# Where the count matrix of the last graph layer is turned: on TensorE, or by the transfer that loads it

## The reference

```python
def _L3_gnn_ref(x, edge_index, W, b):
    row, col = edge_index[0], edge_index[1]
    h = x @ W + b
    agg = segment_sum(h[col], row, num_segments=n)
    deg = segment_sum(ones, row, num_segments=n)
    return agg * where(deg > 0, 1 / deg, 0)[:, None]
...
x = _layernorm(x + _L3_gnn_ref(x, edge_index, W, b))
```

## Time and profile before

| | us |
|---|---|
| three executions, median | 3149.36 |
| profiled execution | 3150.74 |
| its span (first to last instruction) | 3149.1 |
| layers, to the end of the last product of `sum_rows` | 2938.4 |
| seam: from there to the last feature tile | 2938.4 to 2968.2 |
| rest of the last stage, products and turns | 2968.2 to 3143.1 |
| after the last product | 3143.1 to 3149.1 |

### The profile page before, as it was taken

The page is one execution under the profiler, slowest core; times in us unless marked ns, Lnnn a source line. Parts: engine busy times, 40 slices in busy tenths (PEclk is TensorE's granted clock), DMA queues, the critical chain, the costliest instruction groups (busy, mean ns, idle before and its releaser), DMA issues. The chain is left out here.

```text
span 3149.1 us, 65488 instructions
## 1 busy us (share of the span) xinstructions
PE 3043.6 (97%) x17339; PEld 2443.3 (78%) x17340; DVE 2155.6 (68%) x5608; ACT 1528.2 (49%) x3008; POOL 1411.2 (45%) x1629
## 2 busy tenths in 40 slices
PE   7699999999999999999998899999999999999999
PEld 7588888888888888888887666667777888887776
DVE  7788888888888888888886777884555222246523
ACT  2466666666666666666664667770111111111344
POOL 2677777777777777777773322330001000000111
PEclk9899999999999999999999999999999999999999
DMA  5555555555555555555553888887556777678485
GB/s 176 169 164 160 164 161 166 164 164 161 164 163 165 162 164 164 164 163 162 164 164 100 281 275 278 281 280 236 168 180 196 225 221 225 218 230 264 96 127 99
DMA packets 298300, 584.82 MB, mean 186 GB/s; under 512 B 43361, under 2 KB 150842, under 8 KB 298234
## 3 DMA queue, kind: packets, MB, share of 16 engines
q1 hardware_dynamic: 180960, 280.20, 29.6%
q0 software_dynamic: 90416, 254.46, 28.8%
q10 hardware_dynamic: 26858, 49.32, 4.4%
HBM read 493.97 MB, written 110.32 MB: 192 GB/s over the span
## 5 line engine op out<-in xcount | busy, mean ns | idle before, releaser
L985 PE MATMUL bank<-parts,ring 128*128 128x512 f32 x2500 | 621.7, 397 | 4.4 <-DVE T_buf L1770 2.2
L985 PEld LDWEIGHTS bank<-parts,ring 128*128 128x128 f32 x2500 | 460.0, 188 | 105.3 <-issue 5.8
L620 POOL DMA_INDIRECT msgs<-rows_out,sidx x416 | 408.6, 982 | 152.0 <-issue 94.8
L613 POOL DMA_INDIRECT p_in<-p_tab,gidx x416 | 403.7, 970 | 138.8 <-issue 110.1
L613 POOL DMA_INDIRECT q_in<-q_tab,gidx x416 | 398.2, 957 | 126.8 <-issue 125.8
L675 PE MATMUL bank<-hidden1h,w1h 128*108 128x512 f32 x936 | 406.7, 435 | 3.6 <-DVE hidden2l L865 3.6
L675 PE MATMUL bank<-w2h,hidden2h 108*128 108x256 f32 x1248 | 402.5, 322 | 0.0
L676 PE MATMUL bank<-hidden1l,w1h 128*108 128x512 f32 x936 | 368.9, 394 | 0.0
L677 PE MATMUL bank<-hidden1h,w1l 128*108 128x512 f32 x936 | 367.3, 392 | 0.0
L784 ACT ACTIVATE hidden2h<-bank,b1c 108x512 fp32r<-108x512 f32 (+1 forms) x312 | 214.6, 688 | 298.1 <-PE bank L691 298.1
L677 PE MATMUL bank<-w2h,hidden2l 108*128 108x256 f32 x1248 | 351.2, 281 | 0.0
(11 more groups left out here) (253 smaller groups left out, 6073.6 us busy)
## 6 DMA issues: line engine op xcount, KB each, us to landing
ring<-counts SPq DMA_DIRECT2D x500, 320.0 KB, 3.3
R_buf<-msgs SPq DMA_DIRECT2D x544, 130.0 KB, 3.1
counts<-cells ACTq DMA_DIRECT2D x125, 320.0 KB, 3.4
eT<-in_edge_T SPq DMA_DIRECT2D x104, 256.0 KB, 2.9
R_buf<-counts POOLq DMA_DIRECT2D x25, 480.0 KB, 7.1
R_buf<-counts POOLq DMA_DIRECT2D x25, 320.0 KB, 5.8
p_in<-p_tab,gidx POOLq DMA_INDIRECT x416, 3.2
q_in<-q_tab,gidx POOLq DMA_INDIRECT x416, 3.2
```

The costliest lines, as they stand in the source:

```text
L613: pool.indirect_dma_start(out=rows_in[:, z, c], out_offset=None, in_=tab[:], in_offset=bass.IndirectOffsetOnAxis(ap=gidx[:, z, which, c:c ...
L620: pool.indirect_dma_start(out=msgs[:], in_=rows_out[:, z, c], in_offset=None, out_offset=bass.IndirectOffsetOnAxis(ap=sidx[:, z, c:c + 1], ...
L985: mm = pe.matmul(bU[t].rearrange("p (w c) -> p w c", w=2), ring[:, cell(odd, a), t * P:(t + 1) * P].bitcast(dt), parts[k % 2][:, :, a].bit ...
```

## The change

The counts are turned by the transfers, not by PE.

- POOL, during the layers, copies every half row tile of `counts` into a new tensor in HBM, `counts_h`, with float32 made bfloat16 on the way (`shorten`): 50 transfers from HBM to HBM, one for each eight slices of the layers (`PACE` = 8). 15 of them stand ahead of the weights for passes 1 and 2 in POOL's queue, 32 ahead of the weights of the last pass, 3 behind.
- SP, behind its 500 loads, waits for all 50 and issues 25 transposing transfers, one for each row tile: 128 rows of 3200 bfloat16 values to `AT_h`, 128 x 25 x 128, 800 KB, in the place that `rows_b` had. The third waits until the first has been used (`f["ca"]`), and so on.
- ACT makes float32 of the turned bfloat16 rows, SBUF to SBUF, in two copies for each row tile: 12 blocks (1536 columns) and 13 blocks (1664 columns) (`widened`). The first copy of row tile 0 goes into `ring`, which has free places sooner than `parts[1]`.
- PE does products only in the last stage. `TAIL` and `TAIL_ACT` are written anew; `bP`, the two PSUM banks of the products, are exchanged.

```diff
+        counts_h = dram("counts_h", [T * P, NP], BF16)
...
+            AT_h = [R_buf[:, 0:NP].bitcast(BF16)[:, z * NP:(z + 1) * NP].rearrange("p (s n) -> p s n", s=T)
+                    for z in range(2)]
...
-            bT, bP = bU[0:4], [bU[4], bY[1]]
+            CAST = (slice(0, 12), slice(12, T))
+            first_AT = ring[:].rearrange("p s c -> p (s c)")[:, 0:12 * P].rearrange("p (s n) -> p s n", n=P)
...
+            bT, bP = bU[0:4], [bY[1], bU[4]]
...
+            TAIL = [("sum", 0, 0), ("sum", 0, 1), ("turn 2", 0), ("sum", 0, 2), ("weigh 2", 0), ("turn 2", 1),
...
+            TAIL_ACT = [("cast", 0, 0), ("root", 0), ("cast", 0, 1), ("root", 1), ("high", 0), ("root", 2), ("high", 1),
+                        ("cast", 1, 0), ("root", 3), ("high", 2), ("cast", 1, 1), ("root", 4), ("high", 3), ("high", 4)]
...
+                    sp.wait_ge(f_short, 16 * 2 * T)
+                    sp.wait_ge(S["ev"], B * (4 * B - 2))
+                    for n in range(T):
+                        if n >= 2:
+                            sp.wait_ge(f["ca"], n - 1)
+                        sp.dma_start_transpose(AT_h[n % 2], counts_h[n * P:(n + 1) * P, :]).then_inc(f_T[n % 2], 16)
...
+                    def shorten(first, last):
+
+                        for j in range(first, last):
+                            n, at = j // 2, ROW_HALF[j % 2]
+                            pool.wait_ge(S["pc"], PACE * (j + 1))
+                            stand_alone(pool, s_up)
+                            pool.dma_start(counts_h[n * P:(n + 1) * P, :].rearrange("p (b c) -> p b c", b=B)[:, at],
+                                           row_of(n, at)).then_inc(f_short, 16)
+
+                    PACE = 8
+                    shorten(0, 15)
...
+                    shorten(15, 47)
                     pool.wait_ge(S["lin"], 3 * T)
                     stand_alone(pool, s_up)
                     reload(0, slice(0, KD), wview(W3), 12, (KD, D))
...
+                    shorten(47, 2 * T)
...
+                        if dt is F32R:
+                            if q in (0, 3):
+                                pe.wait_ge(f["ev" if q == 0 else "ca"], n + 1)
+                            if isinstance(n, int) and n < 2:
+                                if n == 1 and q == 0:
+                                    pe.wait_ge(S["ev"], B * 4 * B)
+                                pe.wait_ge(S["y"], 3 * T + min(4 * q + 4, T))
...
+                        def body(n, z):
+                            for q in range(QN):
+                                products(n, z, q, AT_exact[z], F32R)
...
+                    def widened(n, z, use, i):
+
+                        if i == 0:
+                            act.wait_ge(f_T[z], 16 * (use + 1))
+                            if isinstance(n, int) and n == 0:
+                                act.wait_ge(S["pc"], T * 4 * B - 2 * B + 3)
+                            elif isinstance(n, int) and n == 1:
+                                act.wait_ge(S["pc"], T * 4 * B)
+                            else:
+                                act.wait_ge(f["mm"], n - 1)
+                        elif isinstance(n, int) and n == 0:
+                            act.wait_ge(S["pc"], T * 4 * B)
+                        to = first_AT if isinstance(n, int) and n == 0 and i == 0 else AT_exact[z]
+                        act.copy(to[:, CAST[i]].bitcast(F32R), AT_h[z][:, CAST[i]]).then_inc(f["ev" if i == 0 else "ca"], 1)
```

More of the change, by code:

```diff
@@ L1335, in build @@
         rstd = sb("rstd", [P, TB])
-        f_A = [[sem(f"f_A{z}{i}") for i in range(2)] for z in range(2)]
-        f_full = sem("f_full")
+        f_T = [sem(f"f_T{z}") for z in range(2)]
+        f_short, f_full = sem("f_short"), sem("f_full")
         with ExitStack() as ac:
@@ L1392, in result @@
                 return bY[0][:, 0:D] if k == 3 else bY[buffer(k, i, stage)]
[L1394 removed]
+            f = {n: sem("f_" + n) for n in "tr ev ca mm vc sq h rd".split()}
             f_o = [sem(f"f_o{i}") for i in range(2)]
@@ L1456, in _ @@
                     reload(0, slice(0, KD), wview(W3), 12, (KD, D))
[L1458 to L1473, removed]
+                    shorten(47, 2 * T)
+                    pool.wait_ge(f_short, 16 * 2 * T)
                 @block.tensor
@@ L1548, in products @@
                             mm.then_inc(f["mm"], 1)
[L1550 to L1558, removed]
-                                           rows_b[z][:, s * P:(s + 1) * P], ident_b[:], start=True, stop=True)
-                        mm.then_inc(f["tr"], 1)
                     def turn_full(n, z, use):
@@ L1582, in last_stage @@
                                 tile_step(3, B - 1, *step)
-                        def body(n, z, use, turns=True, before=range(QN)):
-                            for lead in range(0, QN, 2):
-                                pair = range(lead, min(lead + 2, QN))
-                                for q in pair if turns else []:
-                                    turn(n, z, use, q)
-                                for q in pair:
-                                    if q in before:
-                                        products(n - 1, 1 - z, q, AT_exact[1 - z], F32R)
-                        left = range(EARLY, QN)
-                        body(1, 1, 0, False, left)
-                        body(2, 0, 1, True, left)
-                        body(3, 1, 1)
-                        with pe.Fori(2, T // 2) as h:
-                            body(2 * h, 0, h)
-                            body(2 * h + 1, 1, h)
-                        body(T - 1, 0, T // 2)
-                        for q in range(QN):
-                            products(T - 1, 0, q, AT_exact[0], F32R)
+                        for n in range(2):
+                            for q in range(EARLY, QN):
+                                products(n, n, q, AT_exact[n], F32R)
+                        def body(n, z):
+                            for q in range(QN):
+                                products(n, z, q, AT_exact[z], F32R)
+                        with pe.Fori(1, T // 2) as h:
+                            body(2 * h, 0)
+                            body(2 * h + 1, 1)
+                        body(T - 1, 0)
                     def last_stage_full():
@@ L1705, in last_stage, with body @@
                             tail(step)
[L1706 to L1709 removed]
+                            if step[0] == "cast":
+                                widened(step[1], step[1], 0, step[2])
+                        def body(n, z, use):
                             if not (isinstance(n, int) and n < 2):
[L1711 to L1715 removed]
+                                for i in range(2):
+                                    widened(n, z, use, i)
                                 if not (isinstance(n, int) and n < 3):
@@ L1741, in body @@
                                 turned_out(n, q, AT_full)
+                            act.wait_ge(f_T[z], 16 * (use + 1))
+                            act.sem_inc(f["ca"])
                             root_last(n, z % 2)
```

48 lines of the change are left out of this document (16 added, 32 removed).

## The result

The changed kernel takes 3154.62 us (median of 20 runs, 3150.01 to 3157.60), the kernel before 3149.66 us (20 runs beside it, 3144.72 to 3154.20). The ratio is 1.0015 with a 95% interval of 1.0009 to 1.0022: 5 us slower, where 41 us faster was forecast. That is inside the 0.2% that the prediction called no change, but not zero. The profiled execution of the changed kernel took 3150.01 us (span 3148.2), the lowest of its 20, so its whole must not be set against the other one's; its stages can be.

A forecast was written before the change was run, and what follows sets the result against it. PE was taken to bound the kernel, busy 97% of the span. -42.4 + 0.5 + 0.7 = -41.2 us from 3150.74 gives 3109.5, or 3108.2 beside the median; own range 3102 to 3116, with rivals 3101 to 3180.

The forecast's parts named there:

- the 0.2% that the prediction called no change: Whole kernel: a difference up to about 0.2% (6.3 us) cannot be told from no change; chance 0.04.
- the part on what is added to the layers: Layers: POOL's 50 copies add 0 us, and its weight reloads queued behind them are hidden.
- Rival 2: Layers: dearer HBM to HBM transfers stretch 250 slices by 7%, PE waiting for `ring`; +26 us, 3134; chance 0.05.
- The value 0: Layers: the copies add 0.23 to a DMA share of 0.72 and cost PE 0 us.
- the last weights: Layers: the last weight reload, behind slice 376, comes some 30 slices ahead of its first use; hidden.
- the harder case of four loads at once: Earlier trace near 2871 us: four POOL loads at once, DMA share over 1.1, PE still busy 5.00 and 4.74 of 5 us.
- Transfers in the last stage: Last stage: an 800 KB transposing transfer lands in 5.6 us, like a plain one, and hides behind PE's 5.70.
- The two prices: Transposing transfers, from the skill's pages: 32.7 us per row tile by block price, or 3.1 us at 261 GB/s.
- ACT's copies: Last stage: two copies of 1.48 and 1.58 us, 3.1 to 3.4 us per row tile, off the path.
- Row tile 2: Last stage, after the seam: row tile 2 waits until row tile 0 is summed; +0.5 us once.
- The pace of products: Last stage: 0.228 us per product, 581 products in 132.5 us instead of 174.87; gain 42.4 us.
- The seam: Between layers and products: weighing 1.8 us earlier, a possible second clock fall +2.5; together +0.7 us.

The follow-up runs named there:

- e1: Changed kernel with the first 15 copies to counts_h moved ahead of POOL's first wait; layers 782.7 us against 821.9 for the changed kernel rerun.
- e2: Kernel before with the 50 copies added, unread, the first 15 behind POOL's wait; layers 822.8 us against 777.3, last stage 210.8.
- e3: Kernel before with the 50 copies added, unread, the first 15 ahead of POOL's wait; layers 782.1 us against 777.3, last stage 210.9.
- e5: The kernel of e1 run again; layers 780.6 us, against 822.3 for the changed kernel rerun; whole time ratio 0.999 to the kernel before.
- e9: The kernel of e1 run a third time; layers 781.6 us, whole 3177.33 us, ratio 1.009 to the kernel before.
- e8: e5 with copies due at listed slices, none in the 25 slices behind a pass's border; layers 777.9 us, whole 3177.29 us.
- e10: e8 with masks on two table values instead of comparisons with bounds; 3111.79 us, ratio 0.9882 to the kernel before.
- e7: e5 with each transposing transfer from row tile 2 on issued twice, the second unread; last stage 199.7 us against 172.4, 7.40 us per row tile.
- e11: Kernel before with the same two masks as e10 and nothing else; 3150.06 us, ratio 1.0006 to the kernel before.

## Why the prediction was wrong

**The step that failed** is in the part on what is added to the layers: "POOL's weight reloads wait behind these transfers: the first pair behind slice 120, before its condition (slice 125) is met [...] Hidden." It took each copy to be issued at its own due slice. It asked what stands behind the copies, and did not ask what stands ahead of them. Ahead of them stands the wait for the norm of the first pass. It ends when PE is at slice 143, not 125, so that the 15 due slices 8 to 120 are all past when POOL comes to them, and PE wants the weights only 12 slices later. In place of the "Hidden" the runs showed a wait of 33.7 us and, with what came with it, 38 to 42 us. The trace of before had the number: its list of POOL's waits has

```profile
POOL T_buf L1443 <- DVE T_buf L1798: 247.4, 1, 247.4
```

and an engine that stands for 247 us ahead of an instruction stands as long ahead of one written just in front of it. e1 to e3 show this step alone to be worth 38 to 42 us.

**No rival had it.** Rival 2 lost time in the same stage, but by traffic spread over 250 slices, with PE waiting for `ring`, 26 us. PE waited for `ring` once, 0.9 us, and once, 1.0 us, in the kernel before. With copies at the borders the layers are 3 to 5 us longer (e1, e3, e5, e9), away from them 0.6 and 1.4 us (e8, e10), of which no more than 0.3 arise behind slice 50. The value 0 that the prediction took for spread traffic was nearly right, and so was "Hidden" for the last weights: their load landed in 9.6 us, and PE did not wait for them; it was the harder case of four loads at once that was no bound for fifteen at once with a weight load behind them.

**Transfers in the last stage: right.** 25 of them (ns held on SP's queue, first and last start) and their landing:

```profile
L1441 SPq DMA_TRANSPOSE R_buf<-counts_h x25: 2959/3136/4864, 2963.8 to 3121.8; - x25
...
DMA to landing us min/median/max: 5.1/5.2/7.3
```

The prediction took 5.6 from the earlier trace rows. That a plain transfer may stand for a transposing one had no row behind it; here it held. The two prices between which it could not choose are settled by these rows: 25 blocks land in 5.2 us, and one transfer follows another in 3.70 (e7). The 1309 ns a block of the Trainium skill's page "VectorE: DVE Perf Modes", section "The three transpose paths", must not be multiplied by the blocks of one transfer; that would be 32.7. The 261 GB/s of its page "DMA: Bandwidth & Descriptors", section "Latency and other measured facts", is 18% above what was measured, which decides: 0.82 MB in 3.70 us are 221 GB/s.

**ACT's copies: right.** By width, with count, busy us and mean ns:

```profile
L1684 ACT CAST parts<-R_buf 128x1664 fp32r<-128x1664 bf16 x23 | 36.3, 1578 | 0.0
L1684 ACT CAST parts<-R_buf 128x1536 fp32r<-128x1536 bf16 x23 | 33.9, 1475 | 60.7 <-PE bank L1557 57.2 <-DMA R_buf<-counts_h 3.5
```

The slope from two rows had given 1.58 and 1.48, although neither row reads bfloat16. ACT's idle time ends by PE, not by a DMA, at nearly every row tile: the transfers are early.

**Row tile 2: right.** +0.5 forecast, 0.64 measured, and the same row shows that PE never pauses from there on, for 575 products:

```profile
3005.41 1.67 PE L1557 MATMUL bank<-parts 128*128 128x512 f32 x6 [0.58 <-DVE parts L1838]
3007.72 134.40 PE L1557 MATMUL bank<-parts 128*128 128x512 f32 x575 [0.64 <-ACT parts L1684]
```

**The pace of products: too small by 2%.** 575 products in 134.40 us are, without the last one's 0.39, 574 steps of 0.2335, not 0.228. At that pace 581 products are 135.7 us, not 132.5: a term mis-sized by 3.2 us. The whole stretch is 136.8 where 133.0 was forecast with row tile 2's pause. What failed here is a reading of the earlier trace rows: its 25 weight loads begin with one behind a pause, and the second follows it after 0.11 us; that one short step pulled the mean down. Begun at the second, the row of the kernel before is

```profile
3137.07 5.55 PEld L1545 LDWEIGHTS bank<-parts 128*128 128x128 f32 x24
```

which is 23 steps of 0.233 without the last one's 0.19: the pace of after stood in the trace of before, and the turns were worth that much less. The other row there, 30 products in the layers, is a different loop with a pace of 0.227; why the two differ stays open.

**The seam: right in its mechanism.** The second fall of the clock is there, behind a pause of 2.75 us (columns as in the earlier trace rows):

```profile
3000.00:3002.00 2.00, 2.00 (x9) 1.58 (x8) 1.18 (x3) 0.00 (x0) 0.00 (x0) 0.56 0.00 1
```

The seam is 1.2 us shorter than before; +0.7 was forecast, so its size was off by 1.9. Last stage in all: forecast -41.2, measured -39.2 by the windows. With the layers left whole (e10) the kernel gains 37 us; without them it loses 5.

## What to carry to other kernels

When instructions are put into an engine's program, read first what that engine waited for at this place in the trace of before, and for how long: conditions that come due during that wait are met all at once behind it, and "one every 8 slices" becomes a burst. Then ask which small load that a busy engine needs is written behind the burst in the same queue. Large copies that only have to be done by the end belong ahead of such a wait (38 to 42 us here) and away from the places where weights and biases are loaded (2.4 to 2.8 us here). And before a pace is taken from the mean of a short run, its first steps are looked at one by one.

## What the runs showed of the hardware

- A load of 256 KB issued by POOL behind 15 converting copies (8 of 480 KB and 7 of 320 KB) landed after 36 us, where it takes some 4 us otherwise. Loads of `ring` that SP issued in the same stretch landed in 8.5 us at the median: a burst holds its own queue far more than others.
- A converting copy from HBM to HBM lands in 9.1 us (480 KB) and 7.7 us (320 KB) at the median, bursts counted in, where the loads of the same rows to SBUF had 7.1 and 5.8.
- Issuing one transposing transfer of 128 x 3200 holds SP's queue for 3.14 us (median), a plain load of 320 KB for 0.33. Nothing else was due on SP here; where something is, this counts.
- Comparing two values read from tables with their bounds, as the kernel runs, in the counting phase: PE waits 68.5 us for DVE there instead of 25.9, and the layers begin 65.0 us later (e9 against e10, on two chips whose kernels before agree within 1 us). The 22 us beyond PE's waits were not traced. A mask on the same values costs 0.9 us at the median and 4.7 at most by its interval (e11).
- While PE stood still for 33.7 us the granted clock fell to 0.50, half of 2.4 GHz, and the first products behind it ran at that level (0.79 and 0.63 us for 0.40), for 2.7 us. A window within the stall (columns as in the earlier trace rows), with the DMA engines full:

```profile
2440.00:2450.00 10.00, 0.00 (x0) 0.00 (x0) 0.00 (x0) 0.00 (x0) 0.00 (x0) 0.50 1.15 250
```
